# One more merge of transposed terms on GpSimd, skip weights inside another transfer, and a new order on five engines

## The chip, the cores and the metric

The kernel runs on one core of a Trainium2 chip. It is written instruction by instruction: each of the five engines (PE for matrix products, DVE, ACT and POOL for element-wise work, SP for transfers) has a queue that is written out by hand, and semaphores order the queues against each other. The metric is the device time of one execution in microseconds (us), lower is better. Three executions of the kernel before took 78.17, 78.08 and 77.75 us; the median is 78.08 us.

## The reference

There are two residual blocks on x (8 batches, 128 rows, 256 columns), cut here to what matters:

```python
def xattn(k, v, q, ssm_kernel, D, head_dim):          # k = v = ctx, 16 heads of 8 rows
    kv = einsum('bhil,bhjl->bijhl', k_, v_)           # products of two rows of a head
    y = irfft(rfft(kv, 2 * L) * rfft(ssm_kernel, 2 * L))[..., :L]   # causal convolution along L
    out = y + kv * D                                  # the skip weight of the head
    return einsum('bijhl,bhil->bjhl', out, q_)        # sum over i

x = x + xattn(ctx, ctx, layernorm(x), taps, D, 8)
x = x + down(silu(gate(layernorm(x))) * up(layernorm(x)))    # 256 -> 704 -> 256, integer weights
```

The gate, up and down weights are int32; the zero point 128 is subtracted and each output row has a scale.

## The kernel before, in words

The 16 heads are taken one after another. For a head, the products of its rows of k are made (`all_products` on DVE for the first two heads, `pairs` on POOL and `squares` on ACT for the others), and the convolution is a matrix product on PE with a Toeplitz matrix of the taps (`convolve_across`, L977, and `convolve_within`, L986 and L988). `direct(n)` on DVE (L651) adds the skip weight of the head to the diagonal of its Toeplitz matrix for the first eight heads; for the others the taps themselves get it (`add_skip_to_taps` on POOL, L369) and go out to memory and back (`taps_pad`). DVE multiplies the convolution with q: `multiply_terms(n)`, three instructions (L718, L721, L725), which leaves eight "slots" of terms for each half of a tile of two heads.

x lies in eight tiles of 128 rows. For tile t a first layer norm runs as a chain over three engines: `stats_of_q`, `moments_of_q`, `variance_of_q` on DVE (L663, L667, L671), `root_q` on POOL (L360), `shift_of_q` on DVE (L676), `norm_q` on ACT (L474), `turn_q` on PE (L931, a transpose), `evict_q` on ACT. `sum_terms(t)` on PE (L957) transposes the slots of terms of the tile into one PSUM tile and sums them by accumulation: 8 slots a half for tiles 0 and 1, 4 for tile 2, 2 for tiles 3 to 7. What shortens it are additions ahead: `wrap` on ACT (L499), `merge_front` on POOL (L274), `merge_back` on DVE (L282) and, for tiles 3 to 7, `merge_last` on DVE (L290). Then `add_sum` on DVE (L682) adds the sum to x, and the same kind of norm chain (`stats_of_f`, `moments_of_f`, `variance_of_f`, `root_f`, `shift_of_f`, `norm_f`, `turn_f`) leads into the second part. There `gates(i, t)` on PE (L1010) makes chunk t of the gate and up rows for block i of two tiles, `gate` on ACT (L508) and `hidden_units` on DVE (L733) form the hidden units, `hidden_high` (ACT, L513) and `low` (POOL, or DVE for a few, L258) split them into two parts, and `downs(i, t)` on PE (L1029) multiplies them down. `low_f` (DVE, L704) gives the last part of the input that `gates` reads.

At the start PE does 17 matrix products with zeros (L1049) before the first head. SP issues the transfers of k (`load_k`, L310), the Toeplitz matrices and x (`load_x`, L313); ACT's queue issues the skip weights spread over all partitions (`skip_all`), tile 0 of x, the taps and a second copy of the skip weights (`skip_sb`).

## Time and profile before

| | us |
|---|---|
| median of three executions (lowest, highest) | 78.08 (77.75, 78.17) |
| span of the profiled execution, first to last instruction | 76.7 |
| what lies around the span, if the profiled execution took the median | 1.4 |
| PE busy | 70.7 |
| DVE busy | 63.9 |
| POOL busy | 54.6 |
| ACT busy | 46.7 |

The profiled execution's own time is not listed apart from the three; its span of 76.7 us is what all readings below go by. An engine's busy share can include matrix products that overlap, so the distance from one start to the next is the better measure of what an instruction costs in a queue.

### The profile page before, as it was taken

The page shows a single profiled execution, that of the slowest core. Times are in us where ns is not written, and L with a number is a line of the kernel's source. Part 1 is how long each engine was busy: PE and PEld are TensorE (multiplying, and loading weights), DVE is VectorE, ACT ScalarE, POOL GpSimd, SP SyncE. Part 2 cuts the span into 40 slices and gives each one's busy share as a digit, 9 for nine tenths or more (in the row PEclk, how much of TensorE's full clock was granted, in tenths as well). Part 3 has the DMA queues.
Part 4 walks back from the last instruction along what each step waited for, and adds up shares of the span by engine and source line. Part 5 has one row for each costly group of instructions (what it writes and reads, how often), then busy time and mean ns, then how long its engine had stood idle before and what let it go on. Part 6 is the DMA issues. An engine that isn't in the chain of part 4 may idle for free.

```text
span 76.7 us, 1495 instructions
## 1 busy us (share of the span) xinstructions
PE 70.7 (92%) x469; PEld 57.8 (75%) x469; DVE 63.9 (83%) x191; ACT 46.7 (61%) x115; POOL 54.6 (71%) x73
## 2 busy tenths in 40 slices
PE   4999988879999999999999999999999999999920
PEld 3767735568798777787888797988897989899810
DVE  0088399969999999899999999999999993786760
ACT  0601483275859587976868468746767798766400
POOL 5004798799889599299899949459627899939230
PEclk9999999999999999999999999999999999999995
DMA  0498999999997000000000000000000222200404
GB/s 5 132 256 279 386 344 295 285 384 397 386 353 220 13 0 0 0 0 4 4 9 0 0 0 0 0 0 0 0 9 4 68 68 68 68 9 0 137 0 137
DMA packets 7304, 8.29 MB, mean 108 GB/s; under 512 B 992, under 2 KB 6400, under 8 KB 7296
## 3 DMA queue, kind: packets, MB, share of 16 engines
q1 hardware_dynamic: 6912, 8.00, 31.7%
q10 hardware_dynamic: 384, 0.19, 0.8%
q8 instruction: 4, 0.07, 0.3%
q14 instruction: 4, 0.03, 0.1%
HBM read 7.12 MB, written 1.07 MB: 107 GB/s over the span
## 4 chain that ended last, share of the span: by engine, by line
PE 58%; DMA 15%; DVE 14%; SPq 3%; ACT 3%; issue 2%; DVEq 0%; ACTq 0%
PE conv L1010 18%; PE turn L957 8%; PE down L1029 8%; DMA k_ext<-ctx_ext 8%; DMA toeplitz<-taps 7%; PE conv L977 6%; PE conv L988 6%; PE conv L986 6%; DVE hidden L733 3%; DVE terms L718 2%; PE turn L939 2%; DVE terms L721 2%; PE turn L1029 2%; SPq L310 2%; ACT gate_act L508 1%
## 5 line engine op out<-in xcount | busy, mean ns | idle before, releaser
L1010 PE MATMUL conv<-f_parts,wgu 128*128 128x256 f16 x176 | 21.6, 273 | 0.3
L1010 PEld LDWEIGHTS conv<-f_parts,wgu 128*128 128x128 f16 x176 | 16.7, 98 | 3.5 <-DVE hidden L733 0.8
L376 POOL TENSOR_TENSOR products<-k_ext 128x512 f32<-128x512 f32 (+1 forms) x16 | 18.0, 1144 | 0.6 <-DMA k_ext<-ctx_ext 0.6
L508 ACT ACTIVATE gate_act<-conv,sg_sb 128x256 f32<-128x256 f32 (+1 forms) x24 | 11.2, 471 | 4.6 <-PE conv L1010 4.0
L258 POOL TENSOR_TENSOR h_lo<-hidden,h_hi 128x256 fp32r<-128x256 f32 x18 | 12.9, 729 | 1.4 <-ACT h_hi L513 1.3
L733 DVE SCALAR_TENSOR_TENSOR hidden<-conv,su_sb,gate_act 128x256 f32<-128x256 f32 (+1 forms) x24 | 11.3, 479 | 3.1 <-ACT gate_act L508 2.7
L977 PE MATMUL conv<-products,toeplitz 128*128 128x288 f32 x32 | 11.2, 434 | 0.3 <-DVE terms L725 0.3
L365 POOL TENSOR_TENSOR rstd_f<-variance_f,minus_half 128x1 f32<-128x1 f32 x8 | 5.5, 683 | 7.9 <-DVE variance_f L694 7.9
L718 DVE TENSOR_TENSOR terms<-conv,q_ext 128x512 f32<-128x512 f32 x16 | 10.8, 678 | 0.0
L986 PE MATMUL conv<-products,toeplitz 128*128 128x288 f32 x32 | 10.8, 422 | 0.0
L988 PE MATMUL conv<-products,toeplitz 128*128 128x288 f32 x32 | 10.4, 406 | 0.0
L513 ACT ACTIVATE h_hi<-hidden 128x256 fp32r<-128x256 f32 x20 | 8.1, 413 | 3.3 <-DVE hidden L733 3.3
L1029 PE MATMUL down<-wd,h_hi 128*128 128x256 f32 x35 | 9.8, 307 | 0.0
L274 POOL TENSOR_TENSOR terms<-terms 128x512 f32<-128x512 f32 x6 | 8.3, 1379 | 1.4 <-DVE terms L725 1.4
L1029 PE MATMUL down<-wd,h_lo 128*128 128x256 f32 x35 | 8.8, 280 | 0.0
L721 DVE TENSOR_TENSOR terms<-conv,q_ext 128x384 f32<-128x384 f32 x16 | 8.7, 546 | 0.0
L957 PE MATMUL turn<-ident,terms 128*128 128x128 f32 x60 | 8.0, 275 | 0.1
L988 PEld LDWEIGHTS conv<-products,toeplitz 128*128 128x128 f32 x32 | 6.2, 195 | 1.8
L957 PEld LDWEIGHTS turn<-ident,terms 128*128 128x128 f32 x60 | 6.7, 141 | 1.3 <-DVE terms L725 0.5
L474 ACT ACTIVATE q_rows<-x_sb,shift_q,rstd_q 128x256 f32<-128x256 f32 x8 | 4.8, 595 | 4.6 <-DVE shift_q L676 4.6
L986 PEld LDWEIGHTS conv<-products,toeplitz 128*128 128x128 f32 x32 | 6.2, 199 | 1.7
L1029 PEld LDWEIGHTS down<-wd,h_hi 128*128 128x128 f32 x35 | 6.6, 188 | 0.4 <-DVE h_lo L258 0.2
(64 smaller groups left out, 119.8 us busy)
## 6 DMA issues: line engine op xcount, KB each, us to landing
k_ext<-ctx_ext SPq DMA_DIRECT2D x3, 384.0 KB, 6.1
toeplitz<-taps_pad SPq DMA_DIRECT2D x2, 512.0 KB, 7.9
out<-x_sb SPq DMA_DIRECT2D x8, 128.0 KB, 1.7
toeplitz<-taps SPq DMA_DIRECT2D x3, 256.0 KB, 5.3
wg_int<-wg_t SPq DMA_DIRECT2D x1, 704.0 KB, 8.2
wu_int<-wu_t SPq DMA_DIRECT2D x1, 704.0 KB, 9.5
wd_int<-wd_t SPq DMA_DIRECT2D x1, 640.0 KB, 8.6
x_sb<-x SPq DMA_DIRECT2D x1, 512.0 KB, 7.0
```

The lines of the kernel that those rows point to most:

```text
L258: eng.tensor_tensor(low_of(i, t), hidden[up_lanes(t), i % 2, t, :], high_of(i, t), ALU.subtract).then_inc(done, 1)
L376: nc.gpsimd.tensor_tensor(view(products[:, n:n + 1], first * MADE + GROUP, [[MADE, halves], [GROUP, 4], [1, GROUP]]), view(k, 0, [[EXT * B ...
L508: nc.scalar.activation(gate_act[up_lanes(t), i % 2, t, :], gate_of(i, t), ACT.Silu, scale=sg_sb[gate_lanes(t), t:t + 1]).then_inc(gate_act ...
L718: dve.tensor_tensor(view(z, h, [[TERMS, HALVES], [P, 4], [to, GROUP]]), view(y, HALF0, [[COLS, HALVES], [GROUP, 4], [1, GROUP]]), view(q, ...
L721: dve.tensor_tensor(view(z, h + BACK + CHANNEL, [[TERMS, HALVES], [P + SPARE + CHANNEL, 3], [to, GROUP]]), view(y, HALF0 + GROUP, [[COLS, ...
L733: dve.scalar_tensor_tensor(out=hidden[lanes, i % 2, t, :], in0=up_of(i, t), scalar=su_sb[lanes, t:t + 1], in1=gate_act[lanes, i % 2, t, :] ...
L957: done = nc.tensor.matmul(turned[:, c * P:(c + 1) * P], view(z, c * TERMS + slot, [[1, P]]), ident[:, :], is_transpose=True, start=(n == 0 ...
L977: nc.tensor.matmul(conv[BUFFER[n]][:, BANK:BANK + COLS], toeplitz[:, n, P:L], products[:, n, 0:COLS], start=True, stop=False)
L986: nc.tensor.matmul(y[:, BANK:BANK + COLS], within, products[:, n, MADE:MADE + COLS], start=False, stop=True)
L988: nc.tensor.matmul(y[:, HALF0:BANK], within, products[:, n, 0:COLS], start=True, stop=True).then_inc(conv_done, 1)
L1010: done = nc.tensor.matmul(bank_of(i, t)[:, n, :], wgu[:, c, column:column + P], f_parts[:, i % 2, part, c, :], start=(c == 0 and part == 0 ...
L1029: done = nc.tensor.matmul(down_of(i, r), part[:, r * P:(r + 1) * P], wd[:, t, :], start=own, stop=(t == FULL), skip_group_check=True)
```

## The change

1. A constant FULLY_MERGED = 5 and `merge_fully(eng, t)`: for tiles 5 to 7 POOL adds the second of the two slots that are left onto the first (128 x 256 elements), waiting for `merge_last`. `sum_terms` of these tiles transposes one slot a half, and waits for the new semaphore `fully_merged`.
2. The skip weights become the first 16 columns of k's array, so they arrive with the first transfer of k, and column 0 of the taps, which was zero, holds them for `add_skip_to_taps`. Two transfers of ACT's queue go (`skip_all`, `skip_sb`), and two waits with them. The first transfer of k has 208 columns in place of 192.
3. The queues of PE, DVE, ACT and POOL are written in another order, from the first instructions to the last block. ACT issues the transfer of the padded taps after `norm_q(0)` and not ahead of it.

```diff
@@ constants, merge_fully, load_k
+FULLY_MERGED = 5
+        def merge_fully(eng, t):
+            z = terms[:, t % 2, :]
+            first = view(z, 0, [[TERMS, HALVES], [1, P]])
+            wait(eng, all_merged, t + 1 - TWICE_MERGED)
+            eng.tensor_tensor(first, first, view(z, BACK, [[TERMS, HALVES], [1, P]]), ALU.add).then_inc(fully_merged, 1)
             def load_k(first, last, done):
-                sp.dma_start(k_ext[:, first:last], ctx_ext[:, first:last]).then_inc(done, 16)
+                row = HALVES * EXT * B
+                columns = slice(H + first * row if first else 0, H + last * row)
+                sp.dma_start(k_skip[:, columns], ctx_skip[:, columns]).then_inc(done, 16)
@@ scalar queue, first instructions
-            act.dma_start(skip_all[:, :], skip.rearrange("h a -> (h a)").partition_broadcast(P)).then_inc(skip_loaded, 16)
             act.dma_start(x_sb[:, 0, :], x[0:P, :]).then_inc(x_loaded[0], 16)
             act.dma_start(taps_sb[:, :], taps).then_inc(taps_loaded, 16)
-            act.dma_start(skip_sb[:, :], skip).then_inc(taps_loaded, 16)
             nc.scalar.preload_act_table(ACT.Silu)
+            norm_q(0)
             act.wait_ge(taps_ready, 1)
             act.dma_start(taps_pad, taps_sb[:, :]).then_inc(taps_stored, 16)
-            norm_q(0)
+            evict_q(0)
             act.wait_ge(k_loaded[2], 16)
...
             squares(6)
+            evict_q(1)
+            wrap(0)
+            norm_q(2)
             squares(7)
-            evict_q(1)
+            wrap(1)
+            evict_q(2)
+            norm_q(3)
+            convert_gate()
+            wrap(2)
+            evict_q(3)
             act.wait_ge(k_loaded[4], 16)
             squares(8)
-            norm_q(2)
-            wrap(0)
-            evict_q(2)
...
@@ tensor queue, sum_terms
-                else:
+                elif t < FULLY_MERGED:
                     wait(pe, all_merged, t + 1 - TWICE_MERGED)
+                else:
+                    wait(pe, fully_merged, t + 1 - FULLY_MERGED)
-                    slots = TERM_SLOTS if t < UNMERGED else ONCE_SLOTS if t < TWICE_MERGED else TWICE_SLOTS
+                    slots = TERM_SLOTS if t < UNMERGED else ONCE_SLOTS if t < TWICE_MERGED else TWICE_SLOTS if t < FULLY_MERGED else [0]
@@ host side, arrays
+    skip = np.asarray(L0_xattn_D)
+    k = np.concatenate([np.broadcast_to(skip, (P, H)), k], axis=1)
     taps = np.zeros((H, P + L), np.asarray(L0_xattn_ssm_kernel).dtype)
+    taps[:, 0] = skip
```

On DVE's queue the first rows show the new place of tile 0's statistics. Before, the products of the first head stood first (L657 is `all_products`, L651 `direct`, L663, L667 and L671 the statistics of a tile for q, L676 its shift):

```order
L751 MEMSET zeros 128x128
L657 TENSOR_TENSOR products<-k_ext 128x320 x2
L651 SCALAR_TENSOR_TENSOR toeplitz<-anti,skip_all,toeplitz 128x128
L663 BN_STATS stats_q<-x_sb 128x6
L667 BN_AGGR moments_q<-stats_q 128x2
L657 TENSOR_TENSOR products<-k_ext 128x320
L671 TENSOR_SCALAR variance_q<-moments_q 128x1
L651 SCALAR_TENSOR_TENSOR toeplitz<-anti,skip_all,toeplitz 128x128
L657 TENSOR_TENSOR products<-k_ext 128x320
```

Now DVE begins with the statistics of tile 0 (L672, L676, L680), and its shift (L685) stands between the two halves of the first products (L666); the terms of head 0 (L727, L730, L734) come ahead of the `direct` (L660) of heads 2 and 3:

```order
L760 MEMSET zeros 128x128
L672 BN_STATS stats_q<-x_sb 128x6
L676 BN_AGGR moments_q<-stats_q 128x2
L680 TENSOR_SCALAR variance_q<-moments_q 128x1
L666 TENSOR_TENSOR products<-k_skip 128x320
L685 TENSOR_SCALAR shift_q<-moments_q,rstd_q 128x1
L666 TENSOR_TENSOR products<-k_skip 128x320
L660 SCALAR_TENSOR_TENSOR toeplitz<-anti,k_skip,toeplitz 128x128
L666 TENSOR_TENSOR products<-k_skip 128x320 x2
L660 SCALAR_TENSOR_TENSOR toeplitz<-anti,k_skip,toeplitz 128x128
```

What moved is that the first products now stand behind x's tile 0 and not only behind k, and that `direct(2)` no longer stands ahead of the first terms.

On PE the part between heads 3 and 7 of before reads, with L931 a `turn_q` and L957 a `sum_terms`:

```order
L977 MATMUL conv<-products,toeplitz 128x288
L986 MATMUL conv<-products,toeplitz 128x288
L988 MATMUL conv<-products,toeplitz 128x288
L931 MATMUL down<-ident,q_rows 128x128 x2
L957 MATMUL turn<-ident,terms 128x128 x16
L977 MATMUL conv<-products,toeplitz 128x288
L986 MATMUL conv<-products,toeplitz 128x288
L988 MATMUL conv<-products,toeplitz 128x288
L977 MATMUL conv<-products,toeplitz 128x288
L957 MATMUL turn<-ident,terms 128x128 x16
L931 MATMUL down<-ident,q_rows 128x128 x2
```

The same part of the new order (L987, L996 and L998 are a head's convolution, L967 a `sum_terms`, L939 a `turn_q`):

```order
L967 MATMUL turn<-ident,terms 128x128 x16
L987 MATMUL conv<-products,toeplitz 128x288
L939 MATMUL down<-ident,q_rows 128x128 x2
L996 MATMUL conv<-products,toeplitz 128x288
L998 MATMUL conv<-products,toeplitz 128x288
L987 MATMUL conv<-products,toeplitz 128x288
L996 MATMUL conv<-products,toeplitz 128x288
L998 MATMUL conv<-products,toeplitz 128x288
L967 MATMUL turn<-ident,terms 128x128 x16
L939 MATMUL down<-ident,q_rows 128x128 x2
L987 MATMUL conv<-products,toeplitz 128x288
```

The first sum of terms stands ahead of head 4, the turn of tile 2 inside head 4, and the second sum ahead of head 6.

On POOL the stretch from head 14's products to the second block's first `low` was this before (L376 `pairs`, L258 `low`, L274 `merge_front`, L365 `root_f`):

```order
L376 TENSOR_TENSOR products<-k_ext 128x2x256
L258 TENSOR_TENSOR h_lo<-hidden,h_hi 128x256
L274 TENSOR_TENSOR terms<-terms 128x2x2x128
L258 TENSOR_TENSOR h_lo<-hidden,h_hi 128x256
L365 TENSOR_TENSOR rstd_f<-variance_f,minus_half 128x1
L274 TENSOR_TENSOR terms<-terms 128x2x2x128
L376 TENSOR_TENSOR products<-k_ext 128x2x256
L365 TENSOR_TENSOR rstd_f<-variance_f,minus_half 128x1
```

And it is this now, with L297 the new `merge_fully`, L384 `pairs`, L259 `low`, L275 `merge_front` and L373 `root_f`:

```order
L384 TENSOR_TENSOR products<-k_skip 128x2x256
L259 TENSOR_TENSOR h_lo<-hidden,h_hi 128x256
L275 TENSOR_TENSOR terms<-terms 128x2x2x128
L373 TENSOR_TENSOR rstd_f<-variance_f,minus_half 128x1
L297 TENSOR_TENSOR terms<-terms 128x2x128
L384 TENSOR_TENSOR products<-k_skip 128x2x256
L275 TENSOR_TENSOR terms<-terms 128x2x2x128
L259 TENSOR_TENSOR h_lo<-hidden,h_hi 128x256
L297 TENSOR_TENSOR terms<-terms 128x2x128
L373 TENSOR_TENSOR rstd_f<-variance_f,minus_half 128x1
```

Two of the three new additions stand here; the third follows `merge_front` of tile 7.

## Rows read from the trace of the kernel before

**Rows 1.** The page: busy time, then tenths in 40 slices of the span.
```profile
PE 70.7 (92%) x469; PEld 57.8 (75%) x469; DVE 63.9 (83%) x191; ACT 46.7 (61%) x115; POOL 54.6 (71%) x73
...
PE   4999988879999999999999999999999999999920
...
DVE  0088399969999999899999999999999993786760
...
PEclk9999999999999999999999999999999999999995
```
**Rows 2.** The chain that ended last, in order: start us, us, what.
```profile
15.12 0.59 ACT q_rows L474
...
55.14 0.34 DVE f_parts L704
...
55.52 1.92 PE conv L1010 x16
```
**Rows 3.** Timeline of PE: start us, us, form, count, idle before and its releaser.
```profile
4.87 1.30 PE L977 MATMUL conv<-products,toeplitz 128*128 128x288 f32 x2
5.96 1.11 PE L986 MATMUL conv<-products,toeplitz 128*128 128x288 f32 x2
6.91 0.65 PE L988 MATMUL conv<-products,toeplitz 128*128 128x288 f32 x2
...
15.76 0.44 PE L931 MATMUL down<-ident,q_rows 128*128 128x128 f32 x2 [0.68 <-ACT q_rows L474]
...
23.59 1.04 PE L957 MATMUL turn<-ident,terms 128*128 128x128 f32 x8
24.46 0.65 PE L986 MATMUL conv<-products,toeplitz 128*128 128x288 f32 x2
```
**Rows 4.** Transfers issued between 0.5 and 1.2 us: KB each, us to landing.
```profile
x_sb<-x ACTq DMA_DIRECT2D x1, 128.0 KB, 4.0
...
k_ext<-ctx_ext SPq DMA_DIRECT2D x1, 96.0 KB, 2.9
```
**Rows 5.** Timeline of the start, ACT's queue (ACTq) and DVE.
```profile
1.17 0.46 ACTq L532 DMA_DIRECT2D x_sb<-x  x1
...
3.66 0.89 DVE L657 TENSOR_TENSOR products<-k_ext 128x320 f32<-128x320 f32 x2 [2.66 <-DMA k_ext<-ctx_ext]
...
8.90 0.35 DVE L651 SCALAR_TENSOR_TENSOR toeplitz<-anti,skip_all,toeplitz 128x128 f32<-128x128 f32 x1 [1.42 <-DMA toeplitz<-taps]
...
10.25 0.68 DVE L718 TENSOR_TENSOR terms<-conv,q_ext 128x512 f32<-128x512 f32 x1
...
11.51 0.41 DVE L663 BATCH_NORM_STATS2 stats_q<-x_sb 128x6 f32<-128x256 f32 x1
11.84 0.13 DVE L671 TENSOR_SCALAR variance_q<-moments_q 128x1 f32<-128x1 f32 x1
...
19.59 0.41 DVE L682 TENSOR_TENSOR x_sb<-x_sb,turn 128x256 f32<-128x256 f32 x1
```
**Rows 6.** Timeline, 46 to 48 us and 57 to 59 us, PE and DVE.
```profile
46.51 0.60 PE L957 MATMUL turn<-ident,terms 128*128 128x128 f32 x4
47.20 1.05 PE L1010 MATMUL conv<-f_parts,wgu 128*128 128x256 f16 x8
...
57.14 0.69 DVE L290 TENSOR_TENSOR terms<-terms 128x512 f32<-128x512 f32 x1
...
57.89 0.66 PE L957 MATMUL turn<-ident,terms 128*128 128x128 f32 x4
```
**Rows 7.** A group of POOL's instructions: busy us, mean ns.
```profile
L258 POOL TENSOR_TENSOR h_lo<-hidden,h_hi 128x256 fp32r<-128x256 f32 x18 | 12.9, 729 | 1.4 <-ACT h_hi L513 1.3
```
**Rows 8.** Timeline, POOL and DVE: two additions of terms at once, and one alone.
```profile
41.84 0.67 DVE L282 TENSOR_TENSOR terms<-terms 128x512 f32<-128x512 f32 x1
41.85 1.78 POOL L274 TENSOR_TENSOR terms<-terms 128x512 f32<-128x512 f32 x1
...
54.82 1.28 POOL L274 TENSOR_TENSOR terms<-terms 128x512 f32<-128x512 f32 x1 [0.70 <-DVE terms L725]
```

More of the change, by code:

```diff
@@ L413, in _ @@
             pairs(8, 0, 2)
+            root_q(4)
+            merge_front(nc.gpsimd, 2)
+            root_q(5)
+            root_f(0)
             pairs(9, 0, 2)
-            merge_front(nc.gpsimd, 2)
-            root_q(4)
-            root_f(0)
-            root_q(5)
             pairs(10, 0, 2)
@@ L436, in _ @@
             merge_front(nc.gpsimd, 5)
+            root_f(4)
+            merge_fully(nc.gpsimd, 5)
+            pairs(15, 0, 2)
+            merge_front(nc.gpsimd, 6)
             low(0, 4)
-            root_f(4)
-            merge_front(nc.gpsimd, 6)
-            pairs(15, 0, 2)
+            merge_fully(nc.gpsimd, 6)
             root_f(5)
@@ L459, in _ @@
             low(3, 0)
+            add(1, 0)
+            add(1, 1)
             low(3, 2)
@@ L792, in _ @@
             multiply_terms(2)
+            variance_of_q(3)
+            multiply_terms(3)
             dve.wait_ge(x_loaded[3], 16)
             stats_of_q(4)
+            add_sum(0)
+            stats_of_q(5)
             shift_of_q(3)
-            multiply_terms(3)
-            stats_of_q(5)
+            moments_of_q(4)
+            stats_of_f(0)
+            moments_of_q(5)
+            variance_of_q(4)
             multiply_terms(4)
-            add_sum(0)
-            moments_of_q(4)
             multiply_terms(5)
@@ L802, in _ @@
             stats_of_q(6)
-            stats_of_f(0)
-            variance_of_q(4)
-            moments_of_q(5)
-            moments_of_q(6)
-            moments_of_f(0)
             variance_of_q(5)
             add_sum(1)
+            moments_of_f(0)
+            moments_of_q(6)
+            shift_of_q(4)
+            stats_of_f(1)
+            merge_back(dve, 2)
             variance_of_q(6)
+            moments_of_f(1)
+            direct(7)
             variance_of_f(0)
-            merge_back(dve, 2)
@@ L813, in _ @@
-            direct(7)
-            stats_of_f(1)
+            multiply_terms(6)
+            add_sum(2)
+            shift_of_q(5)
+            shift_of_f(0)
             stats_of_q(7)
-            shift_of_q(4)
-            multiply_terms(6)
-            shift_of_f(0)
-            moments_of_f(1)
-            add_sum(2)
             variance_of_f(1)
             multiply_terms(7)
-            shift_of_q(5)
+            stats_of_f(2)
             shift_of_f(1)
-            stats_of_f(2)
+            moments_of_q(7)
@@ L826, in _ @@
+            moments_of_f(2)
             low_f(0)
+            variance_of_f(2)
             multiply_terms(8)
             low_f(1)
-            moments_of_f(2)
+            merge_back(dve, 3)
             multiply_terms(9)
-            merge_back(dve, 3)
+            merge_last(dve, 3)
             dve.wait_ge(scales_loaded, 3 * 16)
             hidden_units(0, 0)
-            variance_of_f(2)
-            merge_last(dve, 3)
+            variance_of_q(7)
+            hidden_units(0, 1)
+            add_sum(3)
@@ L848, in _ @@
+            multiply_terms(11)
+            add_sum(4)
             hidden_units(0, 3)
-            merge_last(dve, 4)
-            multiply_terms(11)
+            stats_of_f(4)
+            hidden_units(0, 4)
             shift_of_q(7)
-            shift_of_f(3)
-            add_sum(4)
+            merge_back(dve, 5)
+            low_f(2)
+            moments_of_f(4)
             multiply_terms(12)
-            low_f(2)
-            stats_of_f(4)
-            merge_back(dve, 5)
-            moments_of_f(4)
@@ L859, in _ @@
-            hidden_units(0, 4)
+            variance_of_f(4)
             low_f(3)
+            merge_last(dve, 5)
+            shift_of_f(4)
             hidden_units(0, 5)
             multiply_terms(13)
-            variance_of_f(4)
-            merge_last(dve, 5)
-            merge_back(dve, 6)
+            low(0, 5)
+            add_sum(5)
             hidden_units(1, 0)
             hidden_units(1, 1)
-            shift_of_f(4)
-            add_sum(5)
             stats_of_f(5)
-            low(0, 5)
+            merge_back(dve, 6)
@@ L1053, in _ @@
             convolve_across(0)
+            pe.wait_ge(ident_ready, 1)
+            turn_q(0, q_ready, 0)
             convolve_within(0)
```

247 lines of the change are left out of this document (116 added, 131 removed).

## The prediction

> **What bounds the kernel now.** I read the page first, then the chain of waits, then PE's and DVE's timelines. The page shows PE busy in nearly every slice after the sixth, and DVE almost as busy [rows 1]. The chain confirms it: from 15.76 us to the end it is mostly a string of matrix products, with one stretch near 55 us where DVE's `low_f` releases `gates` [rows 2]. So there are two nearly full queues. PE's work after its first real product at 4.87 us [rows 3] ends near 73.5 us, and what can shorten the kernel is PE idle time ahead of 15.76 us, PE work, or a later place where PE waits for DVE.
>
> In the start PE stands still for 0.68 us before `turn_q(2)`, waiting for ACT's `norm_q` [rows 3], and the chain shows that this `norm_q` began only at 15.12 us [rows 2]. In ACT's queue it stands behind `squares(8)`, whose data came late. DVE has a hole of 1.42 us at 8.90 us, where `direct(2)` waits for a transfer and the first terms (10.25 us) stand behind it [rows 5].
>
> **The start.** I work out when `sum_terms(2)` can issue, since both orders reach it after nearly the same work; before it was at 23.59 us [rows 3].
>
> Now DVE's queue begins with the statistics of tile 0 of x. Its transfer took 4.0 us from its issue at 1.17 us, second in ACT's queue behind `skip_all` [rows 4, 5]. With `skip_all` gone it is issued one slot (0.44 us) sooner, so I take 0.73 + 4.0 = 4.73 us for its landing. The ends are 3.63 us, if it lands like the 96 KB of k in 2.9 us, and 5.17 us, if nothing is won. I take 4.73 since that row is the same transfer. That is later than the 3.66 us at which DVE starts now [rows 5]; the first product of head 0 on PE needs tile 0's three statistics steps (about 0.8 us) and half a product (0.45 us) and comes at 6.0 us, not 4.87. So this edit alone costs PE 1.1 us.
>
> It is paid back behind it. From 4.73 us DVE has three statistics steps, two halves of products with a wait for POOL's root between them, `direct(0)`, head 1's two halves, `direct(1)` and tile 1's three steps: 4.2 us by the starts of the rows before, so the terms of head 0 start at 8.9 us, against 10.25 [rows 5]. The hole of 1.42 us is gone, because `direct(2)` now comes after these terms, at 10.15 us, and its transfer was there at 8.90 us. From 8.9 us on there are, up to the addition that gates `sum_terms(2)`, six `multiply_terms` at 1.26 us each (10.25 to 11.51), seven statistics at 0.33 (11.51 to 11.84), five `direct` and two `add_sum` (rows of 0.35 and 0.41 us, which in a full queue start 0.25 and 0.32 us apart), some fourteen small steps at 0.09 and the `merge_back` itself [rows 5, 8]: 7.6 + 2.3 + 1.3 + 0.6 + 1.2 + 0.7 = 13.7 us. That gives 22.6 us; 22.75 us with the semaphore.
>
> PE gets there in time: three heads until 11.8 us, turn 1, head 3, the first sum at 13.5 us and no longer behind the turn of 15.76 us [rows 3], heads 4 and 5, the second sum at 18.5 us, heads 6 and half of 7 at 22.4 us. The turn of tile 2 is no longer behind `squares(8)`. So the start gives 23.59 - 22.75 = 0.85 us. Its ends are 1.5 us gained (x lands at 3.63 us, 1.1 us sooner, less what else then ends late) and 1.0 us lost (the clock case below).
>
> The removed transfers carried 8 KB and less; the 8 KB that go into k's first transfer are its price, and I count both as nothing beyond the issue slots. `taps_pad` is now issued after `norm_q(0)`, some 0.5 us later, and SP's queue waits for it with the Toeplitz matrices of heads 8 to 11 and the gate weights behind. They are used only after head 7, past 24.46 us [rows 3], and the transfers already queued keep the transfer engines busy, so it costs nothing; without that cover it would be the same 0.5 us on `gates(0, 0)`.
>
> **The turns.** A `sum_terms` with four products takes 0.44 us of PE: four at the pitch of the row of eight, (24.46 - 23.59) / 8 = 0.109 us [rows 3]. With one slot a half two products are left, 0.22 us. Three tiles: 0.65 us of PE saved. PE's queue is full on both sides of them, so I count all of it; the ends are 0.65 and nothing.
>
> **The added wait.** `merge_fully` is 128 x 256 elements on POOL. The nearest rows are `low`, 0.73 us for the same size [rows 7], and `merge_front`, 1.28 to 1.78 us for twice as much [rows 8]; I take 0.73 and keep 1.23 as the upper end. Behind it in POOL's queue stand `pairs(15)`, `root_f(5)`, and `low` instructions that `downs` waits for. For tiles 5 and 6 the DVE addition before it is done about 0.5 us or more ahead of PE's arrival plus 0.73, so nothing is added. For tile 7 it is not hidden: before, `merge_last` began at 57.14 us, ended at 57.83, and PE's sum issued at 57.89 us, with no slack [rows 6]. Now DVE does both additions without the statistics between, about 0.45 us sooner, and POOL adds 0.73 + 0.1 us. That is 0.4 us of new wait against the 0.22 us saved there.
>
> What also changes is the waiting of PE after 23.59 us. Between 46.95 (46.51 + 0.44) and 47.20 us, and ahead of 55.52 us, PE waited for DVE [rows 2, 6]; such gaps sum to about 1.0 us. With DVE earlier most of them could close (0.7 us gained), while the new order may open others. I take 0.3 us lost for this term, tile 7's 0.4 us included, with ends of 0.7 us gained and 1.0 us lost: a replay leaves out small waits, and the trace before has one in every few microseconds.
>
> The sum is -0.85 - 0.65 + 0.3 = -1.2 us on a span of 76.7 us, and what lies around it stays. From the median that is 78.08 - 1.2 = 76.9 us.
>
> **A rule weighed.** When POOL and DVE both added terms at 41.85 us, POOL's addition took 1.78 us; alone it took 1.28 us [rows 8]. So both at once cost POOL 0.5 us and DVE nothing (0.67 us). The Trainium skill says why this could be: its page GPSIMD Engine Reference, section Key points, has POOL share its SBUF interfaces with DVE, with contention when DVE has two SBUF inputs. By that rule, the trace agrees, and it speaks against the change, since all three new additions are POOL work with two SBUF inputs.
>
> **The rivals.**
>
> *The turns saved come back as waits.* Each new addition meets one of DVE's and takes 0.73 + 0.5 = 1.23 us, and the sums of tiles 5 to 7 wait for it: 0.5 us at each, 1.5 us, less the slack of tiles 5 and 6, which leaves about 0.9 us. Then the 0.65 us are eaten and 0.3 us more: 78.08 - 0.85 - 0.65 + 0.3 + 0.9 = 77.8 us. For it speaks the row of 1.78 us; against it, that the new order puts `root_f(4)` between the additions of tile 5.
>
> *The low clock lasts longer, and the kernel gets slower.* The page gives a granted clock of nine tenths or more throughout [rows 1], but the first pair of head 0 lasts 1.30 us, the second has 0.95 us from start to start (5.96 to 6.91), and from 6.91 us a pair lasts 0.65 us [rows 3]: PE began at 1.2 GHz and rose to 2.4 GHz after working almost without a gap since 1.05 us. The change puts a gap of 1.3 us (4.65 to 6.0 us) there. If the clock then rises only when heads 0 and 1 are through, their products cost 0.48 us in place of 0.24 for each; the second head's terms, on which DVE's queue stands, come 1.4 us later by that, and 0.4 us more if x has not come sooner. `sum_terms(2)` is then at 22.75 + 1.8 = 24.55 us, 0.96 us late. 78.08 + 0.96 - 0.65 + 0.3 = 78.7 us. It decides from the point where the first fast pair starts later than about 9 us. Against it: PE works on both sides of the gap.
>
> The Trainium skill, page TensorE: Matmul & The Clock Gate, Part 1, has the low clock as the default state that activity ends. By that rule, the trace agrees with a rise after work, and a gap in the first work is what would put it off. No row here has such a gap in the first work.
>
> *The order doesn't do what it says.* x's tile 0 lands at 5.17 us, DVE fills its hole but starts later by the same, and only the turns are left, less tile 7's wait: 78.08 - 0.65 + 0.4 = 77.8 us, with the first rival.
>
> **How the numbers follow.** Forecast, 76.9 us: 0.60. The two cases near 77.8 us: 0.26. The slower case, 78.7 us: 0.14. A time within 0.5% (0.39 us, 77.69 to 78.47) is about what cannot be told from no change. The forecast's own range is 76.2 to 77.6 us, from its terms' ends of half weight. Of the cases near 77.8 us, some 0.06 fall below 77.69; of the slower case 0.02 fall inside. So faster 0.66, same 0.22, slower 0.12. The range for 8 in 10 is 76.1 to 78.2 us.
>
> **What would show it.** Right, if DVE's first terms start near 8.9 us and `sum_terms(0)` near 13.5, if the eight-product sum of tile 2 issues at 22.4 to 23.1 us, and the two-product sums show 0.22 us with gaps under 0.2 us ahead of those of tiles 5 and 6. Wrong, if `norm_q(0)` or `turn_q(1)` are late, if PE's first fast pair comes after 9 us, if a `merge_fully` takes over 1.1 us, or if a gap over 0.5 us stands ahead of a product after 25 us.

## The result, and the profile after

The changed kernel takes 80.09 us (79.80 to 80.34, four runs) against 78.12 us for the kernel before on the same chip (77.75 to 78.31, four runs). The ratio is 1.0259, with a 95% interval of 1.021 to 1.0309. It is slower by 2.0 us; the forecast was 1.2 us faster, and the time lies outside the range. Ratios here leave out executions that ran over 1.5% above the fastest of their kernel; medians and ranges are of all executions.

The page of the changed kernel: busy times, tenths of PE, and PE's group of the sums of terms.

```profile
PE 70.1 (90%) x463; PEld 56.8 (73%) x463; DVE 66.7 (86%) x191; ACT 46.5 (60%) x115; POOL 57.9 (74%) x76
...
PE   4998989999999999299889999999998999999930
...
L967 PE MATMUL turn<-ident,terms 128*128 128x128 f32 x54 | 7.5, 277 | 2.3 <-DVE terms L291 1.7
```

The reader is to see three things beside [rows 1]. PE has six instructions fewer and 0.6 us less work, as the change says. DVE has the same 191 instructions and 2.8 us more busy time. And PE's tenths have a 2 in the 17th slice (31.1 to 33.0 us), where before there was a 9. The group of the sums of terms shows what that hole waited for: 1.7 us for L291, which is `merge_last` on DVE.

The granted clock is nine tenths or more in every slice, as before except for the last slice there [rows 1], so nothing of this loss is the clock.

The profiled executions show only part of the loss. The span here is 77.7 us, where the three other executions of the changed kernel have 78.0 to 78.5 us; the 76.7 us of the kernel before is longer than the 76.1 us that is the median of its 63 executions measured beside the experiments. So the rows that follow account for 1.0 us of the 2.0 us at the end of the span.

The start went as forecast or a little better. PE's timeline of the changed kernel, as in [rows 3]:

```profile
4.71 1.33 PE L987 MATMUL conv<-products,toeplitz 128*128 128x288 f32 x2
...
7.36 0.65 PE L998 MATMUL conv<-products,toeplitz 128*128 128x288 f32 x2
...
13.27 1.91 PE L967 MATMUL turn<-ident,terms 128*128 128x128 f32 x16
...
22.41 1.07 PE L967 MATMUL turn<-ident,terms 128*128 128x128 f32 x8 [0.19 <-issue]
...
32.89 0.66 PE L967 MATMUL turn<-ident,terms 128*128 128x128 f32 x4 [1.46 <-DVE terms L291]
...
59.19 0.44 PE L967 MATMUL turn<-ident,terms 128*128 128x128 f32 x2 [0.33 <-POOL terms L297]
```

`sum_terms(2)` issues at 22.41 us, 1.2 us ahead of [rows 3]. At 32.89 us the sum of tile 3 has waited 1.46 us. The sum of tile 7 stands at 59.19 us, where it stood at 57.89 us [rows 6], so between 22 and 59 us the kernel loses 1.18 + 1.30 = 2.5 us. PE's last matrix product, first before and then in the changed kernel:

```profile
73.18 0.28 PE L1029 MATMUL turn<-wd,h_tail 128*128 128x256 f32 x1
```

```profile
74.16 0.28 PE L1039 MATMUL turn<-wd,h_tail 128*128 128x256 f32 x1
```

From the sum of tile 2 to there it is 49.59 us before and 51.75 us now.

Why `merge_last(3)` is late can be read where POOL and DVE are laid side by side. Timeline of the changed kernel, 28.8 to 34 us, of both engines:

```profile
28.80 1.29 POOL L275 TENSOR_TENSOR terms<-terms 128x512 f32<-128x512 f32 x1
28.81 1.83 DVE L283 TENSOR_TENSOR terms<-terms 128x512 f32<-128x512 f32 x1
...
31.01 1.27 POOL L384 TENSOR_TENSOR products<-k_skip 128x512 f32<-128x512 f32 x1
...
31.82 1.01 DVE L291 TENSOR_TENSOR terms<-terms 128x512 f32<-128x512 f32 x1
32.25 0.99 POOL L368 TENSOR_TENSOR rstd_q<-variance_q,minus_half 128x1 f32<-128x1 f32 x1
...
33.21 1.27 POOL L275 TENSOR_TENSOR terms<-terms 128x512 f32<-128x512 f32 x1
...
33.93 1.10 DVE L283 TENSOR_TENSOR terms<-terms 128x512 f32<-128x512 f32 x1
```

POOL's addition begins 10 ns ahead of DVE's. It takes its 1.29 us as if alone; DVE's takes 1.83 us, which is POOL's 1.28 us and then DVE's own time. At 31.82 and 33.93 us DVE again comes second and lasts until POOL has ended, plus 0.5 to 0.6 us. In [rows 8] it was the other way round: DVE's addition began 10 ns ahead of POOL's, took 0.67 us, and POOL's took 1.78 us. Whoever starts first holds, and the other stands: a DVE addition of this size then ends 0.5 to 0.6 us after POOL's instruction, and one of POOL's about 1.1 us after DVE's. Where the two starts are within some 20 ns, as in both these cases, the recorded starts alone don't say who will win (one case below went the other way); where they were further apart, they did in the meetings of instructions of 64 x 256 elements or more. POOL's roots of 128 x 1 elements are an exception. They are lengthened when DVE is ahead, but don't lengthen DVE's addition when they are ahead themselves, as POOL and DVE at 37 us of the kernel before show:

```profile
37.25 0.55 POOL L365 TENSOR_TENSOR rstd_f<-variance_f,minus_half 128x1 f32<-128x1 f32 x1 [0.28 <-DVE variance_f L694]
```

```profile
37.48 0.68 DVE L290 TENSOR_TENSOR terms<-terms 128x512 f32<-128x512 f32 x1
```

The two groups of DVE's additions, grouped by shape, first of the kernel before:

```profile
L282 DVE TENSOR_TENSOR terms<-terms 128x512 f32<-128x512 f32 x6 | 4.1, 680 | 0.0
L290 DVE TENSOR_TENSOR terms<-terms 128x512 f32<-128x512 f32 x5 | 3.4, 686 | 0.0
```

The same two groups of the changed kernel:

```profile
L283 DVE TENSOR_TENSOR terms<-terms 128x512 f32<-128x512 f32 x6 | 6.4, 1059 | 0.0
L291 DVE TENSOR_TENSOR terms<-terms 128x512 f32<-128x512 f32 x5 | 4.2, 850 | 0.1
```

Eleven instructions that were not touched take 10.6 us in place of 7.5. That is 3.1 us on a queue that is nearly full, and it covers DVE's whole growth. The busy time of an engine can grow by another engine's work.

### The profile page after: what moved, and what is told of

The parts are those of the page before. It is cut to its first block, busy times and chain, and to the rows that moved or that the text cites. A ratio compares the mean times of both kernels' runs of the same rounds, so it can differ in the third digit from the quotient of the medians.

```text
span 77.7 us, 1484 instructions
## 1 busy us (share of the span) xinstructions
PE 70.1 (90%) x463; PEld 56.8 (73%) x463; DVE 66.7 (86%) x191; ACT 46.5 (60%) x115; POOL 57.9 (74%) x76
## 4 chain that ended last, share of the span: by engine, by line
PE 50%; DVE 32%; DMA 7%; issue 4%; SPq 2%; ACT 1%; POOL 1%; DVEq 0%; ACTq 0%
PE conv L1020 14%; PE down L1039 7%; DMA toeplitz<-taps 7%; PE turn L967 7%; PE conv L987 6%; PE conv L996 6%; PE conv L998 6%; DVE hidden L742 4%; DVE terms L291 4%; DVE terms L727 4%; DVE terms L730 4%; DVE terms L283 3%; DVE x_sb L691 2%; PE turn L947 2%; PE turn L1039 2%
## 5 line engine op out<-in xcount | busy, mean ns | idle before, releaser
L1020 PE MATMUL conv<-f_parts,wgu 128*128 128x256 f16 x176 | 22.1, 273 | 0.0
L384 POOL TENSOR_TENSOR products<-k_skip 128x512 f32<-128x512 f32 (+1 forms) x16 | 18.1, 1148 | 3.1 <-DMA k_skip<-ctx_skip 3.1
L259 POOL TENSOR_TENSOR h_lo<-hidden,h_hi 128x256 fp32r<-128x256 f32 x18 | 13.4, 758 | 3.1 <-ACT h_hi L524 3.0
L987 PE MATMUL conv<-products,toeplitz 128*128 128x288 f32 x32 | 11.2, 434 | 0.0
L996 PE MATMUL conv<-products,toeplitz 128*128 128x288 f32 x32 | 10.6, 414 | 0.3 <-DVE toeplitz L660 0.3
L727 DVE TENSOR_TENSOR terms<-conv,q_ext 128x512 f32<-128x512 f32 x16 | 10.8, 678 | 0.0
L998 PE MATMUL conv<-products,toeplitz 128*128 128x288 f32 x32 | 10.4, 406 | 0.0
L967 PE MATMUL turn<-ident,terms 128*128 128x128 f32 x54 | 7.5, 277 | 2.3 <-DVE terms L291 1.7
L967 PEld LDWEIGHTS turn<-ident,terms 128*128 128x128 f32 x54 | 6.0, 141 | 4.1 <-DVE terms L291 2.2
L730 DVE TENSOR_TENSOR terms<-conv,q_ext 128x384 f32<-128x384 f32 x16 | 8.7, 546 | 0.0
L275 POOL TENSOR_TENSOR terms<-terms 128x512 f32<-128x512 f32 x6 | 8.4, 1393 | 0.1
L996 PEld LDWEIGHTS conv<-products,toeplitz 128*128 128x128 f32 x32 | 6.0, 199 | 2.0 <-POOL products L384 0.7
L998 PEld LDWEIGHTS conv<-products,toeplitz 128*128 128x128 f32 x32 | 6.1, 190 | 1.7
L1039 PEld LDWEIGHTS down<-wd,h_lo 128*128 128x128 f32 x35 | 6.6, 189 | 0.1
```

The source lines that it names most:

```text
L259: eng.tensor_tensor(low_of(i, t), hidden[up_lanes(t), i % 2, t, :], high_of(i, t), ALU.subtract).then_inc(done, 1)
L384: nc.gpsimd.tensor_tensor(view(products[:, n:n + 1], first * MADE + GROUP, [[MADE, halves], [GROUP, 4], [1, GROUP]]), view(k, 0, [[EXT * B ...
L727: dve.tensor_tensor(view(z, h, [[TERMS, HALVES], [P, 4], [to, GROUP]]), view(y, HALF0, [[COLS, HALVES], [GROUP, 4], [1, GROUP]]), view(q, ...
L730: dve.tensor_tensor(view(z, h + BACK + CHANNEL, [[TERMS, HALVES], [P + SPARE + CHANNEL, 3], [to, GROUP]]), view(y, HALF0 + GROUP, [[COLS, ...
L967: done = nc.tensor.matmul(turned[:, c * P:(c + 1) * P], view(z, c * TERMS + slot, [[1, P]]), ident[:, :], is_transpose=True, start=(n == 0 ...
L987: nc.tensor.matmul(conv[BUFFER[n]][:, BANK:BANK + COLS], toeplitz[:, n, P:L], products[:, n, 0:COLS], start=True, stop=False)
```

## The experiments

Ratios are to runs of the kernel before on the same chip. Each expectation was written before its run.

**The skip weights alone** (`skip_only`): the arrays, transfers and waits of part 2, in the old order, without the third addition.

```diff
...
-            act.dma_start(skip_all[:, :], skip.rearrange("h a -> (h a)").partition_broadcast(P)).then_inc(skip_loaded, 16)
-            act.dma_start(skip_sb[:, :], skip).then_inc(taps_loaded, 16)
...
+                sp.dma_start(k_skip[:, columns], ctx_skip[:, columns]).then_inc(done, 16)
...
```

> The kernel before in its own order, with the skip weights inside k's first transfer and in column 0 of the taps, and ACT's two transfers gone. Theory A (DVE's additions of terms wait for POOL's running instruction, 2.8 us more DVE busy time in the changed kernel): the skip edit is not the cause, 77.9 to 78.3 us. Theory B (about 1 us of the loss lies around the span, and comes from the changed transfers): 79.0 us or more, with the distance between time and span 1 us larger than that of the kernel before. Theory C (the third addition's wait on PE is the cause): 77.9 to 78.3 us.

Measured: 77.88 us against 77.81, ratio 1.001 [0.9981, 1.0038]. This part costs and gives nothing by itself.

**The third addition alone** (`third_only`): part 1 in the old order.

```diff
...
             root_f(4)
+            merge_fully(nc.gpsimd, 5)
...
             pairs(15, 0, 2)
+            merge_fully(nc.gpsimd, 6)
...
             merge_front(nc.gpsimd, 7)
+            merge_fully(nc.gpsimd, 7)
```

> The kernel before in its own order and with its own transfers, with the third addition on POOL alone for tiles 5 to 7, behind root_f(4), pairs(15) and merge_front(7), and one turn a half. Theory A: two-product sums save 0.65 us of PE, waits for POOL cost about as much; 77.8 to 78.7 us, with DVE's additions of terms still near 0.68 us each. Theory B: as A. Theory C: 79.5 us or more, since the PE waits for the added link at each of three sums.

Measured: 79.03 us (78.80 to 79.37), ratio 1.0177 [1.0138, 1.0217]: 1.2 us slower, more than any of the expectations but the dearest, and less than that. PE's timeline of this kernel has the three sums that the addition shortens:

```profile
46.84 0.44 PE L970 MATMUL turn<-ident,terms 128*128 128x128 f32 x2 [0.34 <-POOL terms L298]
...
51.12 0.44 PE L970 MATMUL turn<-ident,terms 128*128 128x128 f32 x2 [0.70 <-POOL terms L298]
...
59.09 0.44 PE L970 MATMUL turn<-ident,terms 128*128 128x128 f32 x2 [0.78 <-POOL terms L298]
```

They wait 0.34 + 0.70 + 0.78 = 1.82 us for the addition that saves them 0.65 us. The difference is the 1.2 us measured. In this order DVE's additions of terms all take 0.67 to 0.71 us, and the three new additions 0.72 to 0.82 us, so the additions are not long. At tiles 6 and 7 each begins just behind DVE's `merge_last` (50.35 and 58.31 us), and PE is there by then. Another DVE instruction with two SBUF inputs, `low` for the last part of a block, met POOL (in the kernel before, the same one takes 0.67 us). DVE and POOL at 48 us:

```profile
47.98 1.28 POOL L384 TENSOR_TENSOR products<-k_ext 128x512 f32<-128x512 f32 x1
48.23 1.31 DVE L260 TENSOR_TENSOR h_tail<-hidden,h_tail 64x256 fp32r<-64x256 f32 x1
```

**The start of the new order alone** (`start_only`): the new order up to `turn_q(5)` on PE, `low_f(1)` on DVE, `high_f(1)` on ACT and `pairs(11)` on POOL, then the rest in the old order; no third addition.

```diff
-FULLY_MERGED = 5
+FULLY_MERGED = 99
...
             pairs(11, 0, 2)
+            root_q(6)
+            merge_front(nc.gpsimd, 3)
             pool.wait_ge(k_loaded[5], 16)
             pairs(12, 0, 2)
-            merge_front(nc.gpsimd, 3)
             root_f(2)
             pairs(13, 0, 2)
-            root_q(6)
             merge_front(nc.gpsimd, 4)
...
```

> The changed kernel's order and transfers up to gates(0, 1) and turn_q(5) on PE (up to low_f(1) on DVE, high_f(1) on ACT, pairs(11) on POOL), then the order of before, without the third addition. Theory A: gates(0, 0) near 29.3 us, 1.15 us ahead of before, then the old order, whose additions of terms do not meet POOL's work; 76.9 to 77.4 us. Theory B: the same inside the span, 1 us more around it: 77.9 to 78.4 us. Theory C: 76.9 to 77.4 us.

Measured: 79.26 us (78.73 to 79.40), ratio 1.019 [1.0146, 1.0235]. My theory then, that behind the new start the old order's additions would meet nothing (76.9 to 77.4 us), fell. The start of this kernel is early (`sum_terms(2)` at 22.67 us), and time is lost where the old order begins again. The profiled execution is the fastest of the four, 0.5 us below the median, so its rows show a part of the loss. POOL and DVE there:

```profile
31.80 1.82 POOL L384 TENSOR_TENSOR products<-k_skip 128x512 f32<-128x512 f32 x1
31.82 0.68 DVE L291 TENSOR_TENSOR terms<-terms 128x512 f32<-128x512 f32 x1
32.42 1.76 DVE L283 TENSOR_TENSOR terms<-terms 128x512 f32<-128x512 f32 x1
33.59 1.72 POOL L275 TENSOR_TENSOR terms<-terms 128x512 f32<-128x512 f32 x1
```

Two DVE additions follow one another. POOL loses to the first (1.82 us, though its recorded start is 20 ns ahead), the second then loses to POOL (1.76 us), and POOL's next to it (1.72 us).

**The new order without the third addition** (`after_no_third`).

```diff
-FULLY_MERGED = 5
+FULLY_MERGED = 99
...
-            merge_fully(nc.gpsimd, 5)
...
```

> The changed kernel in its new order, without the third addition: two turns a half for tiles 5 to 7 as before. Theory A: the loss stays, 79.8 to 80.5 us, with additions of terms on DVE of 1.0 to 1.8 us for tiles 3 to 5. Theory B: the same. Theory C: the loss goes, 78.5 us or less.

Measured: 79.66 us, ratio 1.0242 [1.0204, 1.028]. So most of the loss, 1.85 of 2.0 us, is there without the third addition. The same meeting is in its trace: both additions are recorded at 29.77 us, and DVE's takes 1.84 us.

**`merge_back(3)` put back behind head 9's terms** (`after_back3`), as it stood before the change.

```diff
-            merge_back(dve, 3)
             multiply_terms(9)
+            merge_back(dve, 3)
```

> The changed kernel with one line of DVE's queue moved: merge_back(3) behind multiply_terms(9), where it stood before. Theory A (a DVE addition of terms waits until POOL's running instruction ends): the row of 1.83 us goes, but the addition then meets root_f(2) or pairs(12), 0.7 to 1.3 us; the time falls by 0.3 to 1.0 us against the changed kernel, to 79.1 to 79.8 us. Theory D (the additions are long because POOL and DVE work on the same tile of terms): the addition is back at 0.68 us and the time falls by 1.1 us or more.

Measured: 79.37 us over six runs (78.46 to 80.88), ratio 1.0144 [1.0091, 1.0197]. By the ratios it is about 0.9 us better than the changed kernel and far from cured. The profiled execution is the fastest of the six. DVE's additions in it and the POOL instruction beside the second:

```profile
29.36 0.70 DVE L283 TENSOR_TENSOR terms<-terms 128x512 f32<-128x512 f32 x1
29.85 1.34 POOL L384 TENSOR_TENSOR products<-k_skip 128x512 f32<-128x512 f32 x1
30.16 1.57 DVE L291 TENSOR_TENSOR terms<-terms 128x512 f32<-128x512 f32 x1
```

The meeting moved to the next addition.

**The same move in the kernel before** (`before_early3`).

```diff
+            merge_back(dve, 3)
             multiply_terms(9)
-            merge_back(dve, 3)
```

> The kernel before with one line of DVE's queue moved: merge_back(3) ahead of multiply_terms(9). It then starts near 30.0 us, just after POOL's pairs(11) (29.82 us, 1.28 us long, on other tiles). Theory A: the addition lasts until pairs(11) is over and then its own 0.6 us, 1.6 to 1.9 us in all, and the kernel is 0.4 to 1.2 us slower than before, 78.2 to 79.0 us. Theory D: 0.68 us, and the time of before, since the two engines are on different tiles.

Measured: 78.41 us (78.36 to 78.69), ratio 1.0084 [1.0054, 1.0113]. One DVE addition moved ahead makes the kernel before 0.65 us slower by the ratio, and the trace has a meeting with a POOL instruction that works on other data:

```profile
29.31 1.28 POOL L376 TENSOR_TENSOR products<-k_ext 128x512 f32<-128x512 f32 x1
29.54 1.60 DVE L282 TENSOR_TENSOR terms<-terms 128x512 f32<-128x512 f32 x1
```

29.31 + 1.28 - 29.54 = 1.05 us of POOL's time is left when DVE starts, and 0.55 us follow. So the two engines need not work on the same array for it.

**The two engines by themselves** (`port`): six phases of six instructions of 128 x 512 elements each on DVE and POOL, with different arrays, nothing else running: DVE alone, POOL alone, both adding from two SBUF arrays, then POOL adding beside DVE's product of a PSUM and an SBUF array, then beside DVE's statistics, and last POOL's fill beside DVE's addition.

```diff
+            for n, op in enumerate((two_sbuf, None, two_sbuf, one_psum, stats, two_sbuf)):
...
+            for n, op in enumerate((None, two, two, two, two, one)):
```

> Only the two engines, on scratch tiles of 128 x 512 numbers, no part of the reference is computed: six phases of up to six instructions each. In order: DVE's addition of two SBUF tiles alone; POOL's addition of two SBUF tiles alone; both at once; DVE's product of a PSUM tile and an SBUF tile beside POOL's addition; DVE's statistics of one SBUF tile beside POOL's addition; DVE's addition of two SBUF tiles beside POOL's fill. Theory A: in phase 3 the instructions alternate, each start delayed by the other's, and DVE's last up to 1.8 us; in phases 4, 5 and 6 both keep the durations of phases 1 and 2. Theory D: phase 3 as phases 1 and 2, since no tile is shared.

DVE's phases in the timeline, each row a phase (its busy time is the sum of six):

```profile
2.56 3.70 DVE L46 TENSOR_TENSOR vo<-va,vb 128x512 f32<-128x512 f32 x6
...
13.79 9.03 DVE L46 TENSOR_TENSOR vo<-va,vb 128x512 f32<-128x512 f32 x6 [7.40 <-POOL po L71]
24.05 3.68 DVE L49 TENSOR_TENSOR vo<-ps,vb 128x512 f32<-128x512 f32 x6 [1.22 <-POOL po L71]
31.56 3.66 DVE L52 BATCH_NORM_STATS2 vs<-va 128x6 f32<-128x512 f32 x6 [3.83 <-POOL po L71]
39.07 3.70 DVE L46 TENSOR_TENSOR vo<-va,vb 128x512 f32<-128x512 f32 x6 [3.86 <-POOL po L71]
```

Windows of the phases (us; DVE busy, POOL busy):

```profile
13.70:23.00 9.30, 9.03 (x6) 9.17 (x6) 1.00 0.00 0
23.90:31.50 7.60, 3.68 (x6) 7.41 (x7) 1.00 0.00 0
31.50:39.00 7.50, 3.66 (x6) 7.37 (x6) 1.00 0.00 0
```

Alone six DVE additions take 3.70 us and six of POOL's 7.35 us (6.3 to 13.7 us). Beside each other they take 9.03 and 9.17 us: the two take turns. A DVE product with one PSUM input (3.68 us) and DVE statistics with one input (3.66 us) leave POOL's six at 7.41 and 7.37 us, and beside POOL's fill DVE's additions take their 3.70 us. The product, the statistics and the fill were not run alone here. The Trainium skill, page GPSIMD Engine Reference, section Key points, has the contention with DVE instructions with two SBUF inputs; by that rule, the trace agrees.

**One wait on POOL, in the hybrid** (`start_guard`): `start_only`, with POOL's `pairs(13)` held back until DVE's `merge_back(4)` is done.

```diff
+            wait(pool, back_merged, 3)
             pairs(13, 0, 2)
```

> start_only with one wait more: POOL's pairs(13) waits until DVE's merge_back(4) is done, so that POOL and not DVE stands. Theory A: merge_back(4) falls from 1.76 to 0.68 us, DVE gains 1.1 us there, POOL loses 0.4 us; 0.4 to 1.1 us faster than start_only (79.26), 78.2 to 78.9 us. If start_only's loss has another cause (theory E: in most executions the new start itself is slower than in the profiled one), no change from 79.3 us.

Measured: 77.12 us (76.99 to 77.18), ratio 0.9901 [0.9867, 0.9935]. One wait takes 2.1 us from `start_only` by the medians, and this is the fastest kernel by median of this study, though its interval overlaps those of the kernels with waits below. Where `start_only` has 1.76 us:

```profile
31.66 0.69 DVE L283 TENSOR_TENSOR terms<-terms 128x512 f32<-128x512 f32 x1
...
32.49 1.28 POOL L384 TENSOR_TENSOR products<-k_skip 128x512 f32<-128x512 f32 x1 [1.41 <-DVE terms L283]
```

POOL now stands still for 1.41 us. Its next addition, of 33.73 us, ends at 35.01 us, where in `start_only` it ends at 35.31 us, but this profiled execution was 0.76 us ahead before the wait could act (`sum_terms(2)` at 21.91 us against 22.67 us). Counted from there POOL ends 0.46 us later, and PE reaches its last product 0.96 us sooner. The two profiled executions thus show about 1 us of the gain as the work of the wait.

**More of the same** (`start_guard2`): POOL's `root_f(2)` ahead, and `pairs(12)` behind the same wait.

```diff
+            root_f(2)
+            wait(pool, back_merged, 3)
             pool.wait_ge(k_loaded[5], 16)
             pairs(12, 0, 2)
-            root_f(2)
-            wait(pool, back_merged, 3)
             pairs(13, 0, 2)
```

> start_guard with a second arrangement on POOL: root_f(2) stands ahead, and pairs(12) and pairs(13) both stand behind DVE's merge_back(4) by the wait that is already there. Theory A (the engine whose instruction with two SBUF inputs starts first holds, the other stands until it has ended): merge_back(3) falls from 1.10 to about 0.68 us, root_f(2) to about 0.55, and POOL's merge_front(4) ends at about the same time as in start_guard: 76.6 to 76.9 us against 77.12. Rival (POOL's later products become what PE waits for, the head turns of tiles 12 and 13 start late): 77.1 to 77.6.

Measured: 78.66 us (78.27 to 79.97), ratio 1.0061 [1.0029, 1.0093], 1.2 us worse by ratio than `start_guard`; a miss, and the rival named too little. The addition that was to be shortened is (0.68 us at 29.92 us), but POOL now has two products to do after the wait:

```profile
36.64 1.21 DVE L291 TENSOR_TENSOR terms<-terms 128x512 f32<-128x512 f32 x1 [0.25 <-POOL terms L275]
```

`merge_front(4)` ends at about 36.6 us and not at 35.0, DVE waits for it, and then meets POOL twice more, at 36.64 us and at 41.54 us (1.10 us).

**Three waits on POOL in the changed kernel** (`after_guard`).

```diff
+            wait(pool, back_merged, 2)
             merge_front(nc.gpsimd, 3)
             root_f(2)
+            wait(pool, all_merged, 1)
             pairs(13, 0, 2)
             root_q(6)
+            wait(pool, back_merged, 3)
             merge_front(nc.gpsimd, 4)
```

> The full changed kernel with three waits more on POOL, each on a counter that DVE already raises: merge_front(3) behind merge_back(3), pairs(13) behind merge_last(3), merge_front(4) behind merge_back(4). Nothing else is changed. Theory A: DVE's three long additions (1.83, 1.01, 1.10 us) come down to about 0.68 to 0.9, some 1.5 us of DVE time ahead of 35 us, and the kernel takes 78.2 to 79.0 us against the changed kernel's 80.09. Rival (the loss lies in the new order itself or in the third addition, not in the meeting of DVE and POOL): 79.6 or more.

Measured: 77.43 us (77.37 to 79.08), ratio 0.9915 [0.9877, 0.9953].

**The first of the three waits only** (`after_first_wait`).

```diff
+            wait(pool, back_merged, 2)
             merge_front(nc.gpsimd, 3)
```

> The changed kernel with only the first of the three waits: POOL's merge_front(3) stands behind DVE's merge_back(3). If meetings go on to the next addition as POOL is late by the wait, merge_back(3) takes 0.68 us but merge_last(3) or merge_back(4) still over 1 us, and the kernel takes 78.6 to 79.4 us, so that the other two waits are worth 1.2 us or more. If the longest meeting (1.83 us) was all that mattered, it takes 77.4 to 77.9 us, like the kernel with three waits.

Measured: 77.45 us (77.09 to 78.42), ratio 0.9933 [0.9897, 0.997]. Of the two cases named beforehand the second came: the meeting did not move on as in `after_back3`, and the whole gain comes with this one wait. DVE's groups of additions and the sum of tile 7 on PE in this kernel:

```profile
L283 DVE TENSOR_TENSOR terms<-terms 128x512 f32<-128x512 f32 x6 | 4.6, 762 | 0.0
L291 DVE TENSOR_TENSOR terms<-terms 128x512 f32<-128x512 f32 x5 | 3.4, 680 | 0.2
```

```profile
31.67 0.66 PE L968 MATMUL turn<-ident,terms 128*128 128x128 f32 x4 [0.20 <-DVE terms L291]
...
57.16 0.44 PE L968 MATMUL turn<-ident,terms 128*128 128x128 f32 x2 [0.31 <-POOL terms L297]
```

The eleven additions are down from 10.6 to 8.0 us, which is 2.6 us, and the kernel is 0.0326 x 78 = 2.5 us faster by the two ratios. In the profiled executions PE gets from the sum of tile 2 (22.45 us) to that of tile 7 in 34.71 us, where the changed kernel needs 36.78 us and the kernel before 34.30 us. POOL's wait cost 0.71 us in its own queue:

```profile
28.84 0.68 DVE L283 TENSOR_TENSOR terms<-terms 128x512 f32<-128x512 f32 x1
...
29.61 1.28 POOL L275 TENSOR_TENSOR terms<-terms 128x512 f32<-128x512 f32 x1 [0.71 <-DVE terms L283]
```

**Three waits, without the third addition** (`guard_no_third`).

```diff
-FULLY_MERGED = 5
+FULLY_MERGED = 99
...
```

> The new order with the three waits on POOL, and without the third addition: the sums of tiles 5 to 7 transpose two slots a half again. It prices the third addition where DVE and POOL no longer meet. Theory (the third addition is paid at the end of tile 7, where the sum waits for POOL, and hidden at tiles 5 and 6): 0.65 us of PE work comes back, about 0.7 us of waits goes, so 77.2 to 77.7 us, no more than 0.3 us from the kernel with the three waits (77.43). Rival (the third addition is worth its PE work, 0.65 us): 77.9 to 78.2 us.

Measured: 77.52 us (77.24 to 78.48), ratio 0.9958 [0.993, 0.9986], against 77.43 us and 0.9915 with the third addition. The two were measured on different chips, each beside the kernel before, and the intervals overlap: in the new order the third addition is worth 0.1 us by the medians and 0.3 us by the ratios, which the noise does not separate from nothing.

## Why the prediction was wrong

**The start: right in size, in part by luck.** The term was -0.85 us, with `sum_terms(2)` at 22.75 us. It issued at 22.41 us, and in eight profiled executions with the new start it lies between 21.68 and 22.67 us (a ninth, of `after_no_third`, was 1.0 us longer than the median of its kernel and has 23.36 us), against 23.08 to 23.59 us in four with the old one. The luck is that two errors cancelled. The transfer of x's tile 0 landed in 2.7 us, at 3.43 us and so 1.3 us sooner than I took and below the lower end that I had given it, and PE's first product came at 4.71 us and not at 6.0. But the first terms came only 0.4 us sooner than forecast, at 8.51 us: DVE's steps between took 5.1 us where I had 4.2 us, with waits of 0.59 us for POOL's root and 0.45 us for a transfer of a Toeplitz matrix. The rival of the low clock did not happen: PE's gap ahead of head 0 did not come, and its first fast pair lies at 7.36 us, before the 9 us from which that case was to decide. Issue and landing in the changed kernel, as in [rows 4]:

```profile
x_sb<-x ACTq DMA_DIRECT2D x1, 128.0 KB, 2.7
```

**The turns: right in size, and paid for where the order is not made for them.** The three sums take 0.22 us less each. In the old order they wait 1.8 us for it (`third_only`), so what the first rival said of the sums was right there and its 0.9 us too small, though not by its mechanism: the additions took 0.72 to 0.82 us and not 1.23 us. In the new order the added waits are small (none over 0.2 us at tiles 5 and 6, 0.33 us at tile 7, where 0.4 us was forecast), and the net is 0.1 to 0.3 us and not clear of noise (`guard_no_third`).

**The step that failed** is in the paragraph on the rule that was weighed: "So both at once cost POOL 0.5 us and DVE nothing". The row was read rightly and taken too far. It showed one of two cases, that in which DVE began first. For DVE's eleven additions of terms it was always so in the kernel before: they all took their 0.68 us. But the other case was in the same trace, at another of DVE's instructions with two SBUF inputs. DVE's `low` of 64 x 256 elements is there four times, here with the shortest, the median and the longest in ns:

```profile
L258 DVE TENSOR_TENSOR h_tail<-hidden,h_tail x4: 420/545/836, 48.5 to 72.0; 64x256 fp32r<-64x256 f32 x4
```

The longest, at 66.75 us, began while POOL's `low` was running and ended 0.28 us after it; the next longest, 0.67 us at 48.48 us, came second to POOL's `pairs` in the same way.

One reason why the additions of terms were spared is visible in POOL's queue of before, which stood idle near 32 us:

```profile
32.80 0.93 POOL L365 TENSOR_TENSOR rstd_f<-variance_f,minus_half 128x1 f32<-128x1 f32 x1 [1.69 <-DVE variance_f L694]
```

POOL waits from 31.1 us for the variance of tile 2. DVE's addition of 31.29 us meets nobody, and that of 32.64 us begins ahead of POOL's root, which pays (0.93 us). This idle time of POOL looked free, and here it kept POOL out of DVE's way. The new order moved both queues: DVE's `merge_back(3)` stands ahead of head 9's terms, POOL's `merge_front(3)` behind `pairs(12)`, and POOL's `root_f(2)` no longer waits for its variance. So POOL works through, and reaches `merge_front(3)` 10 ns ahead of `merge_back(3)`. The idle time is not the only way to spare DVE: in `after_first_wait` POOL stands for 0.71 us once and then works on, and the four DVE additions after it take 0.68 to 0.69 us.

So the price of a meeting for DVE was up to 1.83 - 0.68 = 1.15 us, where I had 0. I had looked for meetings only with the three new additions and only on POOL's side, and none of my rivals had this case. The sign that I had named for being wrong did come, a gap over 0.5 us ahead of a product after 25 us: it is the 1.46 us ahead of the sum of tile 3. The mis-sized term is the last one, "0.3 us lost, ends 0.7 gained and 1.0 lost" for all that happens after 23.59 us; it measured 2.8 us lost. That is the 51.75 - 49.59 = 2.16 us by which PE takes longer from the sum of tile 2 to its last product, and the 0.65 us of turns that are already off it. One meeting at 28.8 us and what follows from it make 2.0 us of this in the traces (with one wait on POOL the same way takes 49.72 us) and 2.5 us in the ratios.

What is shown: that the wait alone moves the kernel from 1.0259 to 0.9933; that DVE's additions of two SBUF arrays take turns with POOL's, and that no other of the tested kinds do; that the same move of one addition makes the kernel before slower. Without the meeting the change gives 0.5 us and not the 1.2 us forecast. In the profiled executions it gives 1.0 us of span (75.7 us against 76.7 us): 1.1 us at the start, 0.65 us of turns, and 0.8 us lost after the start, where 0.3 us was forecast; what this 0.5 us more consists of stays open. The rest of the missing 0.7 us goes mostly with the execution on which the sum was made, whose span was 0.6 us longer than the usual 76.1 us and whose third sum, at 23.59 us, was the latest of its kind.

Open is why one wait is enough. In `after_back3` the meeting moved on, in `after_first_wait` it didn't, though both pull the two merges of tile 3 apart, by about 1.3 us and 0.8 us (counted from the sum of tile 2). Who comes first in the next meeting is decided by less than I can forecast from rows.

## What to carry to other kernels

When POOL and DVE both work on two SBUF inputs, read each meeting in the timeline by who starts first: the second one lasts until the first has ended, plus most of its own time (0.5 to 0.6 of DVE's 0.68 us, 1.1 of POOL's 1.28 us), and for DVE beside a longer POOL instruction that is the dear case. Look for both cases before you call one of them free. An engine's idle time off the critical path can be what keeps it out of another's way; before it is filled, look at what runs beside it. If DVE's short instruction must come first, one wait on POOL for a counter that DVE already raises can do it; in the one case tried, holding back two of POOL's products in place of one cost 1.2 us again.

## What the runs showed that I had not expected

- DVE's addition of 128 x 512 elements takes 0.68 us alone and up to 1.84 us beside POOL; the counterpart is POOL's 1.28 and up to 1.82 us. POOL's smallest instruction of this kind, 128 x 1, goes from 0.55 to about 1.0 us when DVE is ahead, but when it starts ahead of DVE's addition, by 20 ns (0.70 us in `after_back3`) or by 0.2 us (0.68 us before), it delays that by almost nothing.
- The same 128 KB of x landed in 2.6 to 2.9 us in the ten profiled executions without the two transfers of skip weights in ACT's queue, and in 3.8 to 4.0 us in the three with them. Which of the two transfers matters was not tested. `skip_only` (2.7 us, and the time of before) shows that this sooner landing is worth nothing while DVE's queue does not begin with x.
- Adding one semaphore wait to POOL took 2.1 and 2.5 us from the two kernels that had the dear meeting, and left them 0.8 and 0.5 us below the kernel before.
